# Layer 0 attention of a four-layer transformer kernel: single-head scores in two row tiles of TensorE

## The reference

```python
def _L0_attn_ref(x, wq, wk, wv, wo):
    ...
    q, k, v = (proj(wq), proj(wk), proj(wv))          # [B, 32, 256, 16]
    q, k = _apply_rope(q, sin, cos), _apply_rope(k, sin, cos)
    scores = jnp.einsum('bnth,bnsh->bnts', q, k) * (1.0 / math.sqrt(h))
    scores = jnp.where(causal, scores, -jnp.inf)
    attn = jax.nn.softmax(scores, axis=-1)
    out = jnp.einsum('bnts,bnsh->bnth', attn, v)
    out = out.transpose(0, 2, 1, 3).reshape(B, T, C)
    return jnp.einsum('btc,dc->btd', out, wo)
```

## Time and profile before

| | us |
|---|---|
| median of 3 runs (2546.08 to 2551.23) | 2549.92 |
| profiled execution | 2548.08 |
| its span, first to last instruction | 2546.2 |
| PE busy | 2447.2 (96%) |
| PE weight loads busy | 1958.9 (77%) |
| DVE busy | 1614.8 (63%) |
| ACT busy | 1103.3 (43%) |
| POOL busy | 570.1 (22%) |

### The profile page before, as it was taken

The page is one execution under the profiler, slowest core; times in us unless marked ns, Lnnn a source line. Parts: engine busy times, 40 slices in busy tenths (PEclk is TensorE's granted clock), DMA queues, the critical chain, the costliest instruction groups (busy, mean ns, idle before and its releaser), DMA issues. The chain is left out here.

```text
span 2546.2 us, 40914 instructions
## 1 busy us (share of the span) xinstructions
PE 2447.2 (96%) x14448; PEld 1958.9 (77%) x14448; DVE 1614.8 (63%) x2420; ACT 1103.3 (43%) x2158; POOL 570.1 (22%) x423
## 2 busy tenths in 40 slices
PE   6999999999989989999999989999999999999899
PEld 4777777778856668888888878888888877888666
DVE  5796557864477775545444477777777775543576
ACT  3332145442245533123333366666666654323453
POOL 2132200245221225034444300000000023430100
PEclk8999999999989999999999999999999999999999
DMA  2232254222342222234444332322222222322421
GB/s 88 62 114 76 66 105 87 32 44 44 49 100 56 46 32 44 36 116 145 141 146 148 135 101 75 91 91 83 86 63 81 75 38 39 55 46 32 103 61 37
DMA packets 406206, 195.32 MB, mean 77 GB/s; under 512 B 280392, under 2 KB 359728, under 8 KB 406078
## 3 DMA queue, kind: packets, MB, share of 16 engines
q1 hardware_dynamic: 404860, 191.53, 30.2%
q10 hardware_dynamic: 1218, 2.06, 0.3%
HBM read 129.85 MB, written 44.04 MB: 68 GB/s over the span
## 5 line engine op out<-in xcount | busy, mean ns | idle before, releaser
L609 PE MATMUL banks<-xn_hi,w_hi 128*128 128x512 f32 x1264 | 496.0, 392 | 8.5 <-ACT sgf L1152 5.5
L609 PE MATMUL banks<-xn_hi,w_lo 128*128 128x512 f32 x1264 | 492.7, 390 | 0.0
L609 PE MATMUL banks<-xn_lo,w_hi 128*128 128x512 f32 x1264 | 492.7, 390 | 0.0
L609 PEld LDWEIGHTS banks<-xn_hi,w_hi 128*128 128x128 f32 x1264 | 237.7, 188 | 59.9 <-DVE w_lo L597 5.8
L609 PEld LDWEIGHTS banks<-xn_hi,w_lo 128*128 128x128 f32 x1264 | 237.7, 188 | 49.7
L609 PEld LDWEIGHTS banks<-xn_lo,w_hi 128*128 128x128 f32 x1264 | 237.7, 188 | 48.2
L597 DVE TENSOR_TENSOR w_lo<-tw,w_hi 128x512 fp32r<-128x512 f32 (+2 forms) x136 | 115.6, 857 | 201.8 <-ACT w_hi L589 201.7
L2731 DVE TENSOR_SCALAR raw<-banks,cols 128x512 f32<-128x512 f32 x128 | 103.6, 810 | 180.3 <-ACT sq L2714 180.3
L2743 POOL TENSOR_TENSOR ssq<-ssq,sq 128x512 f32<-128x512 f32 x128 | 165.3, 1292 | 183.0 <-ACT sq L2714 183.0
L1273 POOL TENSOR_TENSOR h_lo<-sgf,h_hi 128x512 fp32r<-128x512 f32 (+1 forms) x94 | 128.2, 1368 | 338.3 <-ACT h_hi L1155 338.3
L469 POOL TENSOR_TENSOR nat<-nat,wscale 128x512 f32<-128x512 f32 (+1 forms) x44 | 50.4, 1154 | 651.9 <-DMA nat<-in_L_ffn_w 651.8
(11 more groups left out here) (301 smaller groups left out, 5777.0 us busy)
## 6 DMA issues: line engine op xcount, KB each, us to landing
qk_scratch<-raw SPq DMA_DIRECT2D x64, 512.0 KB, 3.0
qk_raw<-qk_scratch SPq DMA_DIRECT2D x64, 512.0 KB, 3.8
nat<-in_L_ffn_w SPq DMA_DIRECT2D x48, 256.0 KB
head_scratch<-stage SPq DMA_DIRECT2D x16, 512.0 KB, 3.2
st_qs<-st_hi SPq DMA_DIRECT2D x128, 64.0 KB, 2.1
nat<-in_L_attn_Wq SPq DMA_DIRECT2D x32, 256.0 KB
nat<-in_L_attn_Wk SPq DMA_DIRECT2D x32, 256.0 KB
nat<-in_L_attn_Wv SPq DMA_DIRECT2D x32, 256.0 KB
```

Source lines behind the costliest of these rows:

```text
L609: mm = nc.tensor.matmul(to[half][:, :], w[0:n, j, k * P:(k + 1) * P], r, start=first and k == 0 and x == 0, stop=last and k == len(rows) - ...
```

## The change

Layer 0 only. The array is used as two row tiles of 64 rows (`ROW_TILE`): even heads of the pairs in rows 0 to 63, odd heads in rows 64 to 127. Each tile holds the three products of one head (16 rows each, at 0, 16 and 48) and four rows for maxima (at 32). So scores and shifts are done by single heads: `unit_ks` needs no zeros any more and has half the size. `pe_att0` issues a part of the scores in one row tile and a part of a shift in the other, matmul by matmul in turn (`both`), with all waits of both parts in front. The mask is two bf16 matmuls of 64 rows a part. The scores run ahead by half an iteration more, the values are split in two, and the maxima are copied by two instructions of 4 rows each (`copy_tops`). The rows for the maxima must be zero while scores are made: POOL clears `unit_qs` at the start, and later loads bring two small DMAs of zeros. A unit is 12 loads of 16 rows. On SP the units' loads come ahead of the adapters, columns and output weights, which are put between them; on DVE the adapters are turned behind the maxima of parts 3 to 5 and ahead of the reciprocal. The diff, cut:

```diff
-        UNIT_SLOTS, UNIT_LOADS = 3, 9
+        UNIT_SLOTS, UNIT_LOADS, UNIT_ZEROS = 3, 12, 2
...
+            sp.wait_ge(used.sem, s.used0)
+            sp.dma_start(square_f[:, :], t["cst"][:, C_SQUARE:]).then_inc(square_in.sem, 16)
...
-            rows = slice(ROWS, P)
             dve.wait_ge(used.sem, s.used0)
             for stacks in unit_ks:
-                ins = nc.vector.tensor_copy(stacks[rows, :, :, :].rearrange("p j e t -> p (j e) t"),
-                                            tail_bcast(cst[rows, C_NEG:C_NEG + HPC], HALF))
-            ins.then_inc(shift_rows.sem, 1)
+                for e in range(2):
+                    rows = slice(e * ROW_TILE + QUAD, (e + 1) * ROW_TILE)
+                    ins = nc.vector.tensor_copy(stacks[rows, :, :], tail_bcast(cst[rows, C_NEG1:C_NEG1 + PAIRS], HALF))
+                ins.then_inc(shift_rows.sem, 1)
 
         def pool_v0(pool, s):
             pool.wait_ge(used.sem, s.used0)
-            for stacks in unit_ks:
-                nc.gpsimd.memset(stacks[0:ROWS, :, :, :].bitcast(F32), 0.0).then_inc(slot_clear.sem, 1)
+            for slot in range(UNIT_SLOTS):
+                nc.gpsimd.memset(unit_qs[slot][:, :, :].bitcast(F32), 0.0).then_inc(slot_clear.sem, 1)
+            nc.gpsimd.memset(no_tops[:, :].bitcast(F32), 0.0).then_inc(slot_clear.sem, 1)
+            pool.wait_ge(square_in.sem, square_in.count)
+            nc.gpsimd.tensor_copy(square[:, :, :, :].rearrange("p a b n -> p (a b n)"), square_f[:, 0:4 * P])
+            nc.gpsimd.tensor_copy(row64[:, :], square_f[:, 4 * P:]).then_inc(square_ready.sem, 1)
...
+        def unit_load(sp, s, u, kind, e):
+            half, c = divmod(u, QC)
+            slot = u % UNIT_SLOTS
+            src = head_dram["kq".index(kind), c, :, :, :, at(half)].rearrange("j r x t -> r j x t")[e * HD:(e + 1) * HD]
+            for x, part in enumerate((0, 0, 1) if kind == "k" else (0, 1, 0)):
+                rows = slice(e * ROW_TILE + TERM_ROWS[x], e * ROW_TILE + TERM_ROWS[x] + HD)
+                sp.dma_start((unit_ks if kind == "k" else unit_qs)[slot][rows, :, :].bitcast(F32), src[:, :, part, :])\
+                  .then_inc(unit_in[slot].sem, 16)
+        def sp_units(sp, s):
+            for j in range(SLOTS):
+                sp.wait_ge(stage_out[j].sem, in0.st0[j] + 16 * len(PIECES) // SLOTS)
+            for u in range(UNIT_SLOTS):
+                sp.wait_ge(shift_rows.sem, s.neg + u + 1)
+                sp.wait_ge(slot_clear.sem, s.clear + u + 1)
+                for kind in "kq":
+                    for e in range(2):
+                        unit_load(sp, s, u, kind, e)
+        def sp_wo_chunk(sp, wo, m):
+            sp_slot(sp, wo, m)
+            for dst, src in wo.chunks[m]["loads"]:
+                sp.dma_start(dst(m), src).then_inc(loaded[m].sem, 16)
+        def sp_att0(sp, s, wo, adapters):
+            for u in range(UNIT_SLOTS, UNITS):
                 slot = u % UNIT_SLOTS
-                if u < UNIT_SLOTS:
-                    sp.wait_ge(slot_clear.sem, s.clear + u + 1)
-                if u >= UNIT_SLOTS:
-                    sp.wait_ge(shifted.sem, s.sh + 2 * STEPS * (u - UNIT_SLOTS + 1))
-                k, q = (head_dram[x, c, :, :, :, at(half)].rearrange("j r x t -> r j x t") for x in range(2))
-                qs, ks = unit_qs[slot], unit_ks[slot]
-                for x, part in enumerate((0, 1, 0)):
-                    sp.dma_start(qs[x * ST:(x + 1) * ST, :, :].bitcast(F32), q[:, :, part, :]).then_inc(unit_in[slot].sem, 16)
-                for x, part in enumerate((0, 0, 1)):
+                sp.wait_ge(shifted.sem, s.sh + 2 * STEPS * (u - UNIT_SLOTS + 1))
+                sp.wait_ge(slot_clear.sem, s.clear + UNIT_SLOTS + 1)
+                for e in range(2):
+                    rows = slice(e * ROW_TILE + QUAD, e * ROW_TILE + QUAD + PAIRS)
+                    sp.dma_start(unit_qs[slot][rows, :, :].bitcast(F32), bcast(no_tops[0:PAIRS, :].bitcast(F32), PAIRS))\
+                      .then_inc(unit_in[slot].sem, 16)
+                for kind in "kq":
                     for e in range(2):
-                        rows = slice(x * ST + e * HD, x * ST + (e + 1) * HD)
-                        sp.dma_start(ks[rows, :, e, :].bitcast(F32), k[e * HD:(e + 1) * HD, :, part, :])\
-                          .then_inc(unit_in[slot].sem, 16)
+                        unit_load(sp, s, u, kind, e)
+                if u == UNIT_SLOTS + 1:
+                    sp.wait_ge(cleared.sem, 4)
+                    for x in adapters:
+                        adapter_load(sp, x)
+                    sp_columns(sp)
+                if u >= UNIT_SLOTS + 2:
+                    sp_wo_chunk(sp, wo, u - UNIT_SLOTS - 2)
+            sp_wo_chunk(sp, wo, KT - 1)
...
+        def score_heads(part):
+            return (0, part, 0, PAIRS) if part < 2 else (1, part % 2, 2 * (part // 2 - 1), 2)
+        def shift_heads(part):
+            return (0, part % 2, 2 * (part // 2), 2) if part < PAIRS else (1, part % 2, 0, PAIRS)
+        def pe_att0(pe, s):
+            def tile(e, width):
+                return slice(e * ROW_TILE, e * ROW_TILE + width)
+            def both(i, part, j, part2):
+                here, there = inside(i), inside(j)
+                if here:
+                    qt, e, p, n_p = score_heads(part)
+                    n = STEPS * i + part
+                    keys = (qt + 1) * P
+                    slot = att_place(s, i)[2]
+                    if n >= 3:
+                        pe.wait_ge(max_done.sem, s.mx + n - 2)
+                    if i % 2 == 0 and part == 0:
+                        pe.wait_ge(unit_in[slot].sem, s.units[slot] + 16 * (UNIT_LOADS + (UNIT_LOADS + UNIT_ZEROS) * (i // 2 // UNIT_SLOTS)))
+                    if n == 0:
+                        pe.wait_ge(square_ready.sem, square_ready.count)
+                    o = bank[n % 3][:, :].rearrange("p (h k) -> p h k", h=n_p)
+                    q, k = att_queries(s, i), att_keys(s, i)
...
+                if there:
+                    kb, e2, p2_, n_p2 = shift_heads(part2)
+                    m = STEPS * j + part2
+                    if m >= 2:
+                        pe.wait_ge(exp_done.sem, s.ex + m - 1)
+                    if part2 == 0:
+                        pe.wait_ge(top_copied.sem, s.tc + j + 1)
+                    if m == 0:
+                        pe.wait_ge(shift_rows.sem, s.neg + UNIT_SLOTS)
+                    o2 = bank[3 + m % 2][:, :].rearrange("p (h q) -> p h q", h=n_p2)
+                    q2, k2 = att_queries(s, j), att_keys(s, j)
+                for b in range(2):
+                    if here:
+                        nc.tensor.matmul(o[:, :, qt * P + b * ROW_TILE:qt * P + (b + 1) * ROW_TILE], square[tile(e, ROW_TILE), 0, b, :],
+                                         bcast(row64[tile(e, ROW_TILE), :], n_p), start=b == 0, stop=False, skip_group_check=True)
+                    if there:
+                        nc.tensor.matmul(o2[:, :, b * ROW_TILE:(b + 1) * ROW_TILE], square[tile(e2, ROW_TILE), 1, b, :],
+                                         bcast(row64[tile(e2, ROW_TILE), :], n_p2), start=b == 0, stop=False, skip_group_check=True)
+                for x in range(PAIRS):
+                    if here and x < n_p:
+                        mm = nc.tensor.matmul(o[:, x, :], q[tile(e, ROW_TILE), p + x, qt * P:(qt + 1) * P], k[tile(e, ROW_TILE), p + x, 0:keys],
+                                              start=False, stop=x == n_p - 1, skip_group_check=True)
+                        if x == n_p - 1:
+                            mm.then_inc(s_ready.sem, 1)
+                    if there and x < n_p2:
+                        mm = nc.tensor.matmul(o2[:, x, :], k2[tile(e2, ROW_TILE), p2_ + x, kb * P:(kb + 1) * P],
+                                              q2[tile(e2, ROW_TILE), p2_ + x, kb * P:SEQ],
+                                              start=False, stop=x == n_p2 - 1, skip_group_check=True)
+                        if x == n_p2 - 1:
+                            mm.then_inc(shifted.sem, 1)
...
+            for i in range(-3, CHUNKS):
+                for n in range(3):
+                    both(i + 2, 3 + n, i + 1, n)
+                values(i, 0, 0)
+                tops(i + 2)
+                for n in range(2):
+                    both(i + 3, n, i + 1, 3 + n)
+                values(i, 0, 1)
+                values(i, 1, 0)
+                values(i, 1, 1)
+                both(i + 3, 2, i + 1, 5)
 
...
+            for i in range(-3, CHUNKS + 1):
+                for part in range(3, STEPS):
+                    top(i + 2, part)
+                if i == CHUNKS:
+                    dve.wait_ge(pv_done.sem, s.pv + 2 * CHUNKS)
+                    dve_lo(dve, wo, 1, 1, ALL)
+                if i in turns:
+                    dve_adapter(dve, turns[i])
+                    if i == max(turns):
+                        dve_columns(dve)
+                inverse(i - 1)
```

(44 more changed lines are left out.)

119 lines of the change are left out of this document (106 added, 13 removed).

## The result

The changed kernel takes 2559.35 us (median of 15 runs, 2553.3 to 2566.54) where the kernel before takes 2551.9: a ratio of 1.003, 95% interval 1.0021 to 1.004. It is slower by some 7.5 us; 2533.1 was predicted. The profiled execution of after is its slowest run.

What follows compares the result with a forecast made beforehand. PE's pace was taken to bound the stage. Thirteen iterations 1.48 us shorter, prologue +1.6, unit 5 +1, adapters +2.5 and tail -2.7 summed to -16.8: 2533.1 us, range 2527 to 2538 (8 in 10: 2525 to 2546).

Steps and rivals of the forecast that it cites:

- Iteration: One of 13 full iterations of layer 0's attention: 7.25 us instead of 8.73, 1.48 less.
- B4 to B6: Last three of an iteration's six calls of `both`, behind T: 2.2 us, between 1.86 and 3.18.
- B1 to T: From an iteration's first call of `both` to T: 2.7 us, set by DVE's four maxima and two signals.
- T: Turned maxima in an iteration, behind the first eight values; waits for the chunk's sixth maximum and takes 0.31 us.
- B: Rival: the row tiles don't overlap, iteration 8.76 us, kernel 2549 to 2550, no change; chance 0.12.
- C: Rival: each change of row tile exposes part of the drain, iteration 9.9 us, kernel 2564; chance 0.10.
- A: Rival: DVE and ACT take over in the iteration, 7.85 us, kernel 2540; chance 0.21.
- Adapters and tail: DVE's adapters ahead of the reciprocal, two iterations, +2.5 us; iteration 13 to the projection 15.6 instead of 18.3, -2.7.
- Prologue: Opening of the stage: two copies of chunk 0's maxima and a later score part cost +1.6 us.
- the loads: SP's unit loads: 11 us for a unit's transfer, 1 us of waiting in all.
- the term for unit 5: Unit 5's load, behind unit 4's, adapters and columns, lands at +33, wanted at 32.1: one wait of 1 us.
- The 0 for the other units: Loads of the other units have 17.6 us for a transfer of 11, so no wait.

Runs made afterwards that it cites:

- w_warm: Changed kernel with a_wide's loads, columns behind the last output weight, and 18 dummy matmuls where PE waits in the opening; 2535.17 us.
- b_eouter: Kernel before with the change's loads of a unit: twelve of 16 rows, one head's first, instead of nine; 2558.46 us, ratio 1.0038.
- a_wide: Changed kernel with two of a head's three terms in one 32-row load, eight loads a unit, scratch laid out for it; 2544.18 us, ratio 0.9976 to before.
- a_inter: Changed kernel with a unit's twelve loads alternating between even and odd heads; 2551.36 us, ratio 1.0002 to the kernel before.
- a_few: Changed kernel with only 4 of 12 loads for units 3 to 7, part of the scores' input left out; 2535.91 us, ratio 0.994 to before.
- w_pace: Changed kernel with a_wide's loads, columns behind the last output weight, and SP waiting from unit 3 for keys to land before issuing queries; 2542.32 us.

## Why the prediction was wrong

**Iteration: right.** 7.25 was worked out, 7.16 measured. B4 to B6 were taken as 2.2 between 1.86 and 3.18, and are 1.35 + 0.63 = 1.98. By the estimate from the Trainium skill's "TensorE: Matmul & The Clock Gate", Part 3, they were 2.07: the trace agrees with it better than with my 2.2. B1 to T was 2.7 by DVE's four maxima and is 2.93, T 0.11 behind the last one. Rivals B and C fall with the timeline. A is there as up to 0.4 us of waiting for an exponential in most iterations, inside the sum.

**Adapters and tail: right.** +2.5 for the two adapters is 0.85 + 0.91 = 1.8 (8.01 and 8.07 against 7.16 in w_warm). From B1 of iteration 13 to the projection 15.6 was predicted; in w_warm it is 15.6: T at 445.02, B1 2.93 ahead of it at 442.09, the projection at 457.68.

**Prologue: too small.** From the first score matmul to B1 of iteration 0 it is 10.92 us before, 15.12 in after and 14.47 in w_warm, where the clock is full: +4.2 and +3.5 where +1.6 was written.

**The step that failed: the loads.** The prediction took 11 us for a unit's transfer and 1 us of waiting in all: "The other units' loads have two iterations and 3.1, 17.6 us, for 11." and "The output weights are wanted only at iteration 14 and land before: 0." The 11 came from the earlier trace rows, a unit of nine loads of which three had 32 rows, which went at 202 GB/s (351 to 358). The change issues twelve of 16 rows, one head's first; they have the same bytes, and I counted their issues but not their rate. At 117 GB/s unit 3 takes 16 us. b_eouter shows the mis-sized term alone in the kernel before (+8.2 us), a_wide takes most of it out of after (-15 us). With it went the term for unit 5. Its load was to start 22 us behind unit 4's and land 11 later; it started 25.0 behind and landed 16.5 later. The wait is 2.94 in after and 8.84 in a_inter, where 1 was written; in after it is the smaller only because PE comes later, held up by the gaps before. The 0 for the other units was wrong too: PE waits 1.86 for unit 6 and 2.67 for unit 7, and the small loads behind an output weight held SP for 10.00 us at 412.91 and 8.66 at 433.42.

**Two terms that were not in the sum.** PE's idle time without a semaphore, 7.0 us in after: before has no such gap, nor has b_eouter with queues as full. It stands at places 512 records apart, whatever the kernel, with a slow 16 KB instruction transfer in it or just before it; and it goes, but for 0.3 us in a_few, where fewer bytes are queued (a_few, w_pace). That PE's instructions arrive late is the reading that fits all of this. It isn't proved, since no run moved an instruction transfer alone, and it doesn't say why a_inter and w_warm have no such gap. And the clock: the sum has no term for it, since before had 1.00 throughout the stage. After runs at 0.50 for 44 of the stage's 153 us, 17 of them in the opening. As an estimate the 27 others cost half their length, 14 us, which with the 14.5 us of idle time is about the 28.6 us between after's stage and w_warm's.

**The sum as it should have been.** With the loads at before's rate, the columns out of the way and the opening filled, w_warm stands at 2535.2 against the 2533.1 forecast: at the projection it is 14.2 us ahead of before, though it starts its stage 3.7 later. Its stage is 18.0 us shorter than before's, and the forecast had 16.8. That the two lie so near is partly luck: iterations 0.09 shorter than forecast, no wait and a smaller cost of the adapters stand against the prologue. It is also more than the change: another layout in DRAM, later columns and 18 dummy matmuls. The gain predicted was there; the change as written spent more than all of it on its transfers and what followed from them.

Still open is why 16-row loads are slow. A page of the Trainium skill bears on it: "SBUF — State Buffer", Door 1, says that DMA bandwidth goes by how many of 16 ports the partitions reach, four partitions in a row to a port, with partition p and p + 32 on the same one. By that page's 436 GB/s for 16 ports, 16 rows reach four, an estimate of 109 GB/s, and 32 rows eight, 218. The runs agree in the direction only: 118 to 122 where all loads have 16 rows and one head comes first, 161 to 191 with four loads of 32. A mix by these two figures, an estimate again, would give 163 to a_wide and 145 to before's three of 32 and six of 16, which has 198 and is the fastest of all in the window of the table; and the order alone, at 16 rows throughout, moves the rate from 118 to 136. No run here varied the ports without the rows or the order, so it isn't shown as the cause. As a rival it would have been the one to name: by that estimate a unit's 12 x 128 KB take 14 us instead of 11, and unit 5 is late by 4. What is shown is that the form of the loads sets the rate, not why.

## What to carry to other kernels

When a change alters the shape or the order of its transfers, price it by the rate of a row with that shape, not by bytes; where there is none, take half the rate as a bound and ask which wait then ends last. A faster stage shortens the time in which the next loads must land: look at every transfer issued between two units (columns, weights) and put those nobody is waiting for behind. Where PE gets holes in a stretch that had none, add the lower clock behind the longer ones to the bill; cheap matmuls that fill them can pay. Where the profile gives no releaser for a gap, look for its place in the program: a gap at the first use of a load that ends with its last landing is a wait for it, and one that comes back at even distances in the instruction stream is something else.

## What the runs showed of the hardware

- The rate by the shape of a load, all in pieces of 2 KB and with full DMA engines: 178 to 202 GB/s (three of 32 rows and six of 16 to a unit), 161 to 191 (four and four, the same loads in four kernels), 129 to 152 (twelve of 16, the heads in turn), 117 to 133 (twelve of 16, one head first).
- A 16 KB instruction transfer takes 0.88 to 0.96 us with little else in the queues and up to 1.5 to 1.9 with unit loads. With unit loads in the queues PE stood idle 0.6 to 4.0 us inside a run of matmuls that waits for nothing, in six kernels, and only at places 512 of its records apart.
- When PE waits for a load, it starts 0.09 to 0.13 us after the load's last landing (418.94 and 419.03 in after, 381.08 and 381.21 in b_eouter).
- Two tiles of 64 rows run side by side: B4 and B5, fourteen single heads with their masks, take 1.35 us, where the parts one behind the other are 0.97 + 1.24 = 2.21 by the lengths read before.
- In after, gaps of 1.92, 4.05, 2.94 and 1.86 us were followed by 10.2, 6.8, 6.8 and 3.4 us at 1.2 GHz, those of 1.08 and 2.67 by none. In b_eouter one of 5.19 went with 10.2 us.
